# A retention layer with an FP4-quantized linear branch on one core: quantizing the linear weight one tile per body over two groups, and adding two groups' linear output in the last phase

## The chip, the core and the metric

One Trainium2 chip, one of its cores. The metric is the device time of one execution in microseconds, as the median of several. Names in what follows: TensorE (PE in the profile) multiplies, VectorE (DVE) and GpSimd (POOL) work on tiles elementwise, ScalarE (ACT) applies functions, and SyncE (SP) issues all the DMAs of this kernel on one queue, in order.

## What is computed

For x of shape (4, 1024, 1024), taken as 4096 rows of 1024:

```python
xn = layernorm(x)
q, k, v = heads((xn@Wq + bq)*scale), heads(xn@Wk + bk), heads(xn@Wv + bv)   # 16 heads of 64
ret = (q @ k^T) * D            # D: causal, exp(decay * distance)
ret = ret / clip(abs(sum(ret)), 1)
attn = group_norm(ret @ v) * gn_w + gn_b
attention = (silu(xn@Wg + bg) * attn) @ Wo + bo
# linear branch: both operands rounded to FP4 in blocks of 16, with an 8-bit scale per block
linear = dequant(quant_fp4(xn)) @ dequant(quant_fp4(W_f))^T + b_f
out = x + attention + linear
```

The scale of the quantized weight depends on the largest element of the whole weight, so no tile of it can be quantized before all of it has been seen once.

## The kernel before, in words

The 4096 rows are 8 groups of 512 (`GROUP`), and each group is worked in 4 bodies (`CH`). A body of group g does three things side by side. It projects and attends four heads of group g (`project`, `scores`, `state_increments`, `attend_within`, `attend_earlier` on TensorE). It finishes 128 rows of group g-1: the output projection in two halves (`finish_half`, 24 matmuls of 128x512 each) and the linear branch in two halves (`finish_linear`, 8 matmuls each). And it prepares 128 rows of group g+1 (`layernorm`, `quantize_scales`, `quantize_half` on VectorE).

Every engine runs its own program, written out by hand, and semaphores join them. `at(name, phase, body, k)` gives the count that a semaphore has at a point of the program: `PER[name]` holds how often it is raised in the start and in each body of each phase, and `w(name, k)` waits for what was there at the body's start plus k more. The order of the calls in each `body` is the order on that engine.

The phases are START, FIRST (group 0), SECOND (group 1), MIDDLE (groups 2 to 7) and TAIL (4 short bodies that finish group 7). The linear weight is 8 tiles of 128 rows of W_f. Its largest element is found in FIRST. In SECOND each body loads, quantizes and transposes two tiles (`load_f`, `f_scales`, `f_half`, `move_f`), and no body of SECOND has a `finish_linear`, because the weight isn't complete. So the linear branch of group 0 is missing from the rows that SECOND stores. It is added in TAIL: the last group prepares the quantized rows of group 0 a second time (in `xqT[:, 0]`), TensorE multiplies them into the two banks `sc`, SP loads the stored rows of `out` into `xt`, VectorE adds (`late_full`, `late_added`, `late_ready`), and SP stores them again.

On VectorE, where the tiles of SECOND stand among the rest matters. A body of SECOND runs: layernorm, quantization of the rows, `f_scales(0)`, `mask_scores(0)`, `f_half(0)`, `states(0)`, `f_half(1)`, `group_norm(0)`, `f_scales(1)`, `mask_scores(1)`, `f_half(0)`, `states(1)`, an `emit_half`, `group_norm(1)`, `emit_half`, `emit_done`, `f_half(1)`. `mask_scores(u)` releases `state_increments(u)` on TensorE, `states(u)` releases `attend_earlier(u)`, and `group_norm(u)`, through `normalize(u)` on ScalarE, releases `transpose_g(u)`. `group_norm(1)` itself waits for `attend_earlier(1)`, the last work of TensorE in a body of SECOND.

Of the kernel before, what the change touches and what calls it, by code (L numbers as in the profile page):

```python
# [73 lines left out]
START, FIRST, SECOND, MIDDLE, TAIL = range(5)  # L74
BODIES = (0, CH, CH, CH * (GROUPS - 2), CH)
# [7 lines left out]
    "scores_full": (0, 2, 2, 2, 0), "probs_ready": (1, 2, 2, 2, 0),  # L83
    "kq_split": (0, 4, 4, 4, 0), "qdec_ready": (0, 2, 2, 2, 0),
    "attn_full": (1, 2, 2, 2, 0), "gstats": (0, 2, 2, 2, 0), "within": (0, 2, 2, 2, 0), "normed": (1, 2, 2, 2, 0),
    "gated": (1, 2, 2, 2, 0), "y_ready": (1, 2, 2, 2, 0),
    "xn_ready": (4, 1, 1, 1, 0), "xq_ready": (1, 1, 1, 1, 0),
    "xhi_ready": (8, 1, 1, 1, 0), "xlo_ready": (1, 1, 1, 1, 0), "xT_full": (8, 0, 0, 0, 0), "xnT_ready": (8, 0, 0, 0, 0),
    "f_max": (1, 2, 0, 0, 0),
    "res_biased": (0, 0, 1, 1, 1), "out_ready": (0, 0, 1, 1, 1), "late_full": (0, 0, 0, 0, 2), "late_added": (0, 0, 0, 0, 2), "late_ready": (1, 0, 0, 0, 1),  # L90
    "xqf_ready": (0, 0, 2, 0, 0), "xqf_moved": (1, 0, 2, 0, 0), "f_loaded": (0, 2, 2, 0, 0),

    "xq_moved": (1, 1, 1, 1, 0), "x_moved": (1, 2, 2, 2, 0),
    "x_loaded": (1, 1, 1, 1, 1), "res_loaded": (0, 0, 1, 1, 1),
    "out_stored": (1, 0, 1, 1, 1), "late_stored": (1, 0, 0, 0, 1),
    "w_k": (0, 2, 2, 2, 0), "w_v": (0, 2, 2, 2, 0), "w_q": (0, 2, 2, 2, 0), "w_g": (0, 2, 2, 2, 0),

    "step": (23, 82, 128, 84, 0),
# [32 lines left out]
def run_phase(eng, phase, body):  # L131

    if phase == MIDDLE:
        for g in range(GROUPS - 2):
            with eng.Fori(0, CH) as q:
                body(MIDDLE, q + g * CH, g % 2, q, g + 2)
    elif phase == FIRST:
        for i in range(CH):
            body(FIRST, i, 0, i, 0)
    else:  # L140
        group = {SECOND: 1, TAIL: GROUPS}[phase]
        with eng.Fori(0, BODIES[phase]) as i:
            body(phase, i, group % 2, i, group)


def build(nc, a):
    with ExitStack() as ctx:
# [138 lines left out]
        def _(sp):  # L286
            for name in PRIMED_SP:
                sp.sem_inc(s[name], 16)

# [27 lines left out]
            def body(phase, i, parity, q, group):  # L317
                w = waiter(sp, phase, i)
                rows = ds(group * GROUP - GROUP + q * P, P) if phase != FIRST else None

# [47 lines left out]
                if phase == TAIL:  # L368
                    w("attn_full", 0)
                    w("res_biased", 0)  # L370
                    sp.dma_start(late_res, a["x"][rows, :]).then_inc(s["res_loaded"], 16)

                    w("late_stored", 0)
                    sp.wait_ge(s["x_loaded"], at("x_loaded", TAIL, 0, 0))
                    sp.dma_start(xt[:], a["out"][ds(q * P, P), :]).then_inc(s["x_loaded"], 16)
                    w("late_ready", 1)
                    sp.dma_start(a["out"][ds(q * P, P), :], xt[:]).then_inc(s["late_stored"], 16)
                    w("out_ready", 1)
                    sp.dma_start(a["out"][rows, :], res[:]).then_inc(s["out_stored"], 16)
                    return  # L380
                if phase == FIRST:
# [43 lines left out]
                    return  # L425
                w("out_stored", 0)
                sp.dma_start(res[:], a["x"][rows, :]).then_inc(s["res_loaded"], 16)
                if phase == SECOND:
                    w("f_max", 0)
                    load_f(0)  # L430
# [34 lines left out]
            for phase in (FIRST, SECOND, MIDDLE, TAIL):  # L465
# [7 lines left out]
        def _(pool):  # L473
# [78 lines left out]
        def _(act):  # L552
# [185 lines left out]
        def _(dve):  # L738
            for name in PRIMED_DVE:
                dve.sem_inc(s[name], 1)  # L740
            here = {"phase": START, "body": 0, "n": 0, "scale_n": 0}
# [221 lines left out]
            def body(phase, i, parity, q, group):  # L963
# [196 lines left out]
        def _(pe):  # L1160
# [276 lines left out]
```

## Time and profile before

| | before |
|---|---|
| median of 3 runs | 2232.05 us (2230.95 to 2232.88) |
| profiled execution: its own time | 2231.07 us |
| profiled execution: span | 2228.9 us |
| PE busy | 2093.5 us (94%) |
| DVE busy | 1534.4 us (69%) |
| ACT busy, POOL busy | 689.3 us, 641.3 us |
| mean granted TensorE clock | 0.972 |

The span is what the profile covers; the 2.2 us between it and the execution's own time lie around it. PE is the matmul engine, and the shares are averages over phases with different limits. In the page's forty slices PE is at 9 tenths or more from the twelfth slice on, and DVE is at 9 tenths from the eighth to the eleventh, which are the slices of SECOND.

### The profile page before, as it was taken

The numbers are of one execution on the slowest core, as the hardware profiler recorded it, in microseconds if no ns is written. First come the engines' busy times: TensorE is split into PE (matmuls) and PEld (weight loads), VectorE is DVE, ScalarE is ACT, GpSimd is POOL, SyncE is SP. The second block draws the span as 40 slices with busy tenths as digits, with TensorE's granted clock in tenths as the row PEclk, the third lists the DMA queues.
The fourth block names the chain that finished last, engine by engine and source line by source line (L and its number), as shares of the span: only waits on it lengthen the run. The fifth ranks groups of instructions, "written<-read, shape, count | busy, mean of one in ns | idle before, by whom it ended". The sixth has DMA issues, their size and how long they took to land.

```text
span 2228.9 us, 51250 instructions
## 1 busy us (share of the span) xinstructions
PE 2093.5 (94%) x18047; PEld 1066.7 (48%) x18098; DVE 1534.4 (69%) x4379; ACT 689.3 (31%) x1318; POOL 641.3 (29%) x456
## 2 busy tenths in 40 slices
PE   5687888989899999999999999999999999999999
PEld 3343444444454545555545455554554555545444
DVE  8587878999966666666676766666666666666742
ACT  5555451322133223222322322223222322322210
POOL 1222232233232332223332232332332223323321
PEclk8888999999899999999999999999999999999999
DMA  7656733432333332323333233233333322333323
GB/s 309 214 190 219 258 110 95 144 108 91 94 119 118 101 106 90 100 89 104 118 110 109 90 99 108 77 118 118 108 108 90 99 90 94 119 118 99 104 75 123
DMA packets 180244, 269.30 MB, mean 121 GB/s; under 512 B 117184, under 2 KB 117312, under 8 KB 180160
## 3 DMA queue, kind: packets, MB, share of 16 engines
q1 hardware_dynamic: 180160, 268.19, 37.7%
q8 instruction: 51, 0.84, 0.2%
q14 instruction: 33, 0.27, 0.0%
HBM read 201.04 MB, written 37.75 MB: 107 GB/s over the span
## 4 chain that ended last, share of the span: by engine, by line
PE 74%; DVE 17%; DMA 3%; issue 2%; ACT 1%; SPq 1%; POOL 0%; DVEq 0%; ACTq 0%
PE mm L1257 46%; PE mm L1199 7%; PE tp L1199 7%; PE mm L1208 4%; DMA ftile<-in_w_f 2%; PE tp L1267 2%; PE four L1307 2%; PE four L1320 2%; PE tp L1295 1%; DVE xa L807 1%; PE four L1280 1%; DVE xa L808 1%; DVE state L1004 1%; DVE xa L802 1%; DVE wo L896 1%
## 5 line engine op out<-in xcount | busy, mean ns | idle before, releaser
L1257 PE MATMUL mm<-xnT,wring 128*128 128x512 f16 x6144 | 1379.2, 383 | 14.4 <-ACT qT L620 14.1
L1257 PEld LDWEIGHTS mm<-xnT,wring 128*128 128x128 f16 x6144 | 603.1, 99 | 720.3 <-issue 44.1
L651 ACT ACTIVATE work<-four,gs 128x64 f32<-128x64 f32 x512 | 158.5, 414 | 575.5 <-DVE gs L1031 575.5
L512 POOL TENSOR_TENSOR yT<-gn,gate 128x512 f32 (+1 forms) x64 | 82.8, 1293 | 881.2 <-ACT gn L662 881.2
L1018 DVE BATCH_NORM_STATS2 gst<-four 128x6 f32<-128x64 f32 x512 | 73.6, 217 | 215.4 <-PE four L1320 215.4
L1199 PE MATMUL mm<-wo,yT 128*128 128x512 f16 x864 | 194.1, 381 | 0.1
L495 POOL TENSOR_TENSOR qparts<-qT,qparts 128x512 f16<-128x512 f32 x64 | 78.5, 1227 | 372.0 <-ACT qT L620 371.8
L495 POOL TENSOR_TENSOR kparts<-kT,kparts 128x512 f16<-128x512 f32 x64 | 83.0, 1297 | 234.5 <-ACT kT L620 234.5
L1199 PE MATMUL tp<-wo,yT 128*128 128x512 f16 x672 | 149.6, 379 | 0.0
L1199 PEld LDWEIGHTS mm<-wo,yT 128*128 (+1 forms) x864 | 82.3, 98 | 98.7 <-issue 1.9
L620 ACT ACTIVATE vT<-mm,consts,down 128x512 f32<-128x512 f32 x64 | 49.8, 778 | 230.4 <-PE mm L1257 230.4
L618 ACT ACTIVATE qparts<-mm,consts,down 128x512 f16<-128x512 f32 x64 | 49.7, 776 | 226.2 <-PE mm L1257 226.2
L1199 PEld LDWEIGHTS tp<-wo,yT 128*128 (+1 forms) x672 | 65.8, 98 | 79.2
L1208 PE MATMUL mm<-wf,xqT 128*128 128x512 bf16 x368 | 88.4, 381 | 7.6 <-issue 7.6
L618 ACT ACTIVATE kparts<-mm,consts,down 128x512 f16<-128x512 f32 x64 | 50.7, 792 | 140.8 <-PE four L1280 139.5
L807 DVE TENSOR_TENSOR xa<-xa,xm 128x512 f32<-128x512 f32 x80 | 92.1, 1151 | 2.8
L1000 DVE COPY state<-tp 128x65 f32<-128x65 f32 x32 | 7.2, 225 | 117.6 <-PE four L1295 117.6
L1002 DVE COPY state<-carry 128x65 f32 x32 | 8.1, 254 | 116.1 <-PE four L1295 114.1
L502 POOL TENSOR_TENSOR qT<-qT,qfac 128x512 f32<-128x512 f32 x64 | 82.1, 1283 | 11.6 <-POOL qparts L495 11.0
L513 POOL TENSOR_TENSOR gate<-gn,gate 128x512 f32<-128x512 f32 x64 | 83.2, 1300 | 0.0
L620 ACT ACTIVATE gate<-mm,consts,down 128x512 f32<-128x512 f32 x64 | 51.0, 796 | 96.9 <-PE mm L1257 96.9
L1307 PE MATMUL four<-v,probs 64*64 64x65 f32 x2048 | 80.4, 230 | 0.0
(194 smaller groups left out, 2710.5 us busy)
## 6 DMA issues: line engine op xcount, KB each, us to landing
wring<-parts SPq DMA_DIRECT2D x252, 512.0 KB, 3.5
xt<-in_x SPq DMA_DIRECT2D x34, 512.0 KB, 3.6
out<-res SPq DMA_DIRECT2D x32, 512.0 KB, 3.0
parts<-wo SPq DMA_DIRECT2D x28, 512.0 KB, 8.1
res<-in_x SPq DMA_DIRECT2D x28, 512.0 KB, 3.6
ftile<-in_w_f SPq DMA_DIRECT2D x16, 512.0 KB, 4.7
parts<-wring SPq DMA_DIRECT2D x8, 512.0 KB, 7.1
probs<-in_x SPq DMA_DIRECT2D x5, 512.0 KB, 3.8
```

Source lines behind the costliest of these rows:

```text
L495: nc.gpsimd.tensor_tensor(parts[:, 1], full, parts[:, 0], ALU.subtract)\
L502: nc.gpsimd.tensor_tensor(qT[:, u].rearrange("p (c t) -> p c t", c=CH), qT[:, u].rearrange("p (c t) -> p c t", c=CH), factor, ALU.mult).th ...
L512: nc.gpsimd.tensor_tensor(hi, gn[:], gate[:, u], ALU.mult)
L513: nc.gpsimd.tensor_tensor(gate[:, u], gn[:], gate[:, u], ALU.mult).then_inc(s["gated"], 1)
L618: nc.scalar.activation((kparts, None, qparts)[n][:, 0], mm[0][:], ACT.Identity, bias=bias[:, n, pair(u)], scale=down[:, n, pair(u)])
L620: nc.scalar.activation(dst, mm[n % 2][:], ACT.Silu if n == 3 else ACT.Identity, bias=bias[:, n, pair(u)], scale=down[:, n, pair(u)])\
L651: last = nc.scalar.activation(work[:, c * P + h * HD:c * P + (h + 1) * HD], ao[h][:, c * VW:c * VW + HD], ACT.Identity, bias=gs[:, 1, g:g ...
L807: then(V.tensor_tensor(xa[:], xa[:], xm[:], ALU.add))
L1199: last = MM(out[:], y[:, yj, k, ds(q * P, P)], wo[:, wj, k, h * GROUP:(h + 1) * GROUP], start=(n == 0), stop=(n == 3 * KT - 1))
L1208: last = MM(out, xs[:, k, :], wf[:, k, h * GROUP:(h + 1) * GROUP], start=(k == 0), stop=(k == KT - 1))
L1257: last = MM(mm[n % 2][:], wring[:, n, wj, k, :], xnT[:, parity, xj, k, :], start=(j == 0), stop=(j == 3 * KT - 1))
L1307: last = MM(ao[h][tokens(k), columns(k)], probs[tokens(k), h, k // 2, 0:SUB], v1[tokens(k), k // 2, h, :], start=(k < 2), stop=False, skip ...
```

## The change

The weight is quantized one tile per body, over two groups: SECOND (group 1) and a new phase THIRD (group 2); MIDDLE has groups 3 to 7. A body of SECOND or THIRD on VectorE has one `f_scales`, one `f_half(0)` and one `f_half(1)`, at the places that the first tile had, and nothing at those of the second. THIRD has no `finish_linear`, so that group 1 too lacks its linear branch when it is stored. TAIL now adds it for groups 0 and 1. The quantized rows of group 1 are kept for that: SP writes `xqT[:, 1]` (1 MB) to DRAM at the start of SECOND and reads it back after the last body of MIDDLE, into a part of `xnT` that is free by then. A body of TAIL multiplies 16 matmuls into `sc` and 16 into `ao`, and loads, adds and stores two sets of rows, one in `xt` and one in `ftile`. In all, TensorE has as many matmuls as before.

```diff
+START, FIRST, SECOND, THIRD, MIDDLE, TAIL = range(6)
+QUANTIZE = (SECOND, THIRD)
+BODIES = (0, CH, CH, CH, CH * (GROUPS - 3), CH)
...
-"late_full": (0, 0, 0, 0, 2), "late_added": (0, 0, 0, 0, 2), "late_ready": (1, 0, 0, 0, 1),
-"xqf_ready": (0, 0, 2, 0, 0), "xqf_moved": (1, 0, 2, 0, 0), "f_loaded": (0, 2, 2, 0, 0),
+"late_full": (0, 0, 0, 0, 0, 4), "late_added": (0, 0, 0, 0, 0, 4), "late_ready": (2, 0, 0, 0, 0, 2), "late_loaded": (0, 0, 0, 0, 0, 2),
+"xqf_ready": (0, 0, 1, 1, 0, 0), "xqf_moved": (1, 0, 1, 1, 0, 0), "f_loaded": (0, 2, 1, 1, 0, 0),
...
+"out_stored": (1, 0, 1, 1, 1, 1), "late_stored": (2, 0, 0, 0, 0, 2),
...
+late_x = [xqT[:, 0], xnT[:, 1, 0].rearrange("p k t -> p (k t)").bitcast(BF16).rearrange(
+    "p (c k t) -> p c k t", c=CH, k=KT)]
+late_bufs = [xt, ftile]
+late_banks = [sc, ao]
... SP, TAIL
-w("late_stored", 0)
-sp.wait_ge(s["x_loaded"], at("x_loaded", TAIL, 0, 0))
-sp.dma_start(xt[:], a["out"][ds(q * P, P), :]).then_inc(s["x_loaded"], 16)
-w("late_ready", 1)
-sp.dma_start(a["out"][ds(q * P, P), :], xt[:]).then_inc(s["late_stored"], 16)
+for j in range(2):
+    late_rows = a["out"][ds(q * P + j * GROUP, P), :]
+    w("late_stored", j)
+    if j == 0:
+        sp.wait_ge(s["x_loaded"], at("x_loaded", TAIL, 0, 0))
+    sp.dma_start(late_bufs[j][:], late_rows).then_inc(s["late_loaded"], 16)
+    w("late_ready", j + 1)
+    sp.dma_start(late_rows, late_bufs[j][:]).then_inc(s["late_stored"], 16)
... SP, between the phases
+if phase == SECOND:
+    sp.wait_ge(s["xq_moved"], at("xq_moved", SECOND, 0, 0))
+    sp.dma_start(a["xq1"], xqT[:, 1].rearrange("p c k t -> p (c k t)")).then_inc(xq1_kept, 16)
+if phase == THIRD:
+    sp.wait_ge(xq1_kept, 16)
+if phase == TAIL:
+    sp.wait_ge(s["attn_full"], at("attn_full", TAIL, 0, 0))
+    sp.dma_start(late_x[1].rearrange("p c k t -> p (c k t)"), a["xq1"]).then_inc(xq1_back, 16)
... DVE, TAIL
+for j in range(2):
+    w("late_loaded", j + 1)
+    w("late_full", 2 * j + 2)
+    for h in range(2):
+        o = half(late_bufs[j], h)
+        V.scalar_tensor_tensor(o, late_banks[j][h], ffn_scale, o, ALU.mult, ALU.add)\
+         .then_inc(s["late_added"], 1)
+    w("late_added", 2 * j + 2)
+    V.tensor_copy(ls[:, 18:19], ls[:, 15:16]).then_inc(s["late_ready"], 1)
... DVE, bodies that quantize
 group_norm(0)
-if phase == SECOND:
-    f_scales(1)
 mask_scores(1)
-if phase == SECOND:
-    f_half(0)
 states(1)
...
-if phase == SECOND:
+if phase in QUANTIZE:
     emit_half(w, 1, "mm1", 5)
     emit_done(w, "mm1_free", 5)
-    f_half(1)
... PE, TAIL
 pe.wait_ge(s["xq_moved"], i * 16 + at("xq_moved", TAIL, 0, 1 - CH))
-w("late_ready", 0)
-linear(sc[0], 1 - parity, q, 0).then_inc(s["late_full"], 1)
-if last_g:
-    transpose_g(1, 1)
-linear(sc[1], 1 - parity, q, 1).then_inc(s["late_full"], 1)
+pe.wait_ge(xq1_back, 16)
+pe.wait_ge(s["normed"], at("normed", TAIL, 0, 0))
+for j in range(2):
+    w("late_ready", j)
+    for h in range(2):
+        linear(late_banks[j][h], late_x[j], q, h).then_inc(s["late_full"], 1)
+    if last_g and j == 0:
+        transpose_g(1, 1)
 finish_linear(w, parity, q, 0, "mm1", 1)
```

On VectorE, the end of a body of SECOND and the start of the next, where before had the second half of the second tile. Before:

```order
L1138 SCALAR_TENSOR_TENSOR res<-mm,cols,res 128x512 [waits mm1_full]
L1152 COPY ls<-ls 128x1 [waits mm1_free]
L802 TENSOR_TENSOR xa<-ftile,qs 128x512
L751 REGISTER_ALU
L803 TENSOR_SCALAR xa<-xa 128x512 [waits step]
L751 REGISTER_ALU
L805 TENSOR_SCALAR xm<-xa 128x512 [waits step]
```

After:

```order
L1155 SCALAR_TENSOR_TENSOR res<-mm,cols,res 128x512 [waits mm1_full]
L1169 COPY ls<-ls 128x1 [waits mm1_free]
L143 REGISTER_ALU
L143 COMPARE_AND_BRANCH
L143 UNCONDITIONAL_BRANCH
L143 ISA
L790 BN_STATS ls<-xt 128x6 [waits x_loaded]
```

The layernorm of the next body (`BN_STATS`) now follows `emit_done` (the `COPY`) at once; before, the seven operations of `f_half(1)` stood between.

On TensorE, the second body of TAIL (`four` is the tile of the banks `sc` and `ao`). Before:

```order
L1208 MATMUL four<-wf,xqT 128x512 [waits late_ready,xq_moved]
L1208 MATMUL four<-wf,xqT 128x512 x15
L1208 MATMUL mm<-wf,xqT 128x512 [waits xqf_moved,mm1_free]
L1208 MATMUL mm<-wf,xqT 128x512 x7
L1208 MATMUL tp<-wf,xqT 128x512 [waits xqf_moved,t1_free]
L1208 MATMUL tp<-wf,xqT 128x512 x7
```

After:

```order
L1225 MATMUL four<-wf,xqT 128x512 [waits normed,late_ready,xq1_back,xq_moved]
L1225 MATMUL four<-wf,xqT 128x512 x15
L1225 MATMUL four<-wf,xnT 128x512 [waits late_ready]
L1225 MATMUL four<-wf,xnT 128x512 x15
L1225 MATMUL mm<-wf,xqT 128x512 [waits xqf_moved,mm1_free]
L1225 MATMUL mm<-wf,xqT 128x512 x7
```

Sixteen matmuls more, with a wait on `late_ready` of their own ahead of them.

On SP, from the last body of MIDDLE through TAIL. Before:

```order
L345 DMA_TRANSPOSE xqT<-xq 128x8x128
L135 REGISTER_ALU
L135 COMPARE_AND_BRANCH
L142 UNCONDITIONAL_BRANCH
L282 REGISTER_ALU [waits attn_full]
L371 ISA [waits res_biased]
L371 DMA probs<-in_x 128x1024
```

After:

```order
L354 DMA_TRANSPOSE xqT<-xq 128x8x128
L136 REGISTER_ALU
L136 COMPARE_AND_BRANCH
L484 DMA xnT<-xq 128x4096 [waits attn_full]
L143 UNCONDITIONAL_BRANCH
L289 REGISTER_ALU [waits attn_full]
L380 ISA [waits res_biased]
L380 DMA probs<-in_x 128x1024
```

The 1 MB load of the kept rows stands behind the last transposing DMA and ahead of the loads of TAIL.

## Rows read from the trace of the kernel before

**Rows 1.** Busy time by stretch, one body each; columns named, PEclk is the clock.

```profile
core 0: us, PE busy (x) PEld busy (x) DVE busy (x) ACT busy (x) POOL busy (x), PEclk, DMA share, GB/s
316.50:386.70 70.20, 63.81 (x554) 32.42 (x552) 63.26 (x162) 18.58 (x37) 20.96 (x15) 0.95 0.31 91
...
460.40:534.00 73.60, 63.69 (x556) 32.75 (x552) 67.11 (x169) 18.58 (x37) 21.05 (x14) 0.94 0.36 110
...
738.10:802.20 64.10, 63.78 (x559) 32.45 (x560) 41.68 (x125) 18.57 (x37) 19.73 (x14) 1.00 0.33 102
```

**Rows 2.** Timeline of PE, second body of SECOND: start, duration, operation, idle before.

```profile
460.42 11.40 PE L1257 MATMUL mm<-xnT,wring 128*128 128x512 f16 x48
...
499.09 0.28 PE L1295 MATMUL tp<-v,kn 64*64 64x65 f32 x2 [4.63 <-DVE probs L988]
...
532.96 1.15 PE L1320 MATMUL four<-state,qT 64*64 64x65 f32 x32 [5.09 <-DVE carry L1006]
```

**Rows 3.** Timeline of PE, first body of SECOND.

```profile
316.48 10.53 PE L1257 MATMUL mm<-xnT,wring 128*128 128x512 f16 x48
...
350.79 0.28 PE L1295 MATMUL tp<-v,kn 64*64 64x65 f32 x2 [1.13 <-DVE probs L988]
...
371.32 0.65 PE L1229 MATMUL tp<-consts,work 128*128 128x128 f32 x4 [0.89 <-ACT work L651]
```

**Rows 4.** Timeline of PE, third body of MIDDLE.

```profile
738.11 10.52 PE L1257 MATMUL mm<-xnT,wring 128*128 128x512 f16 x48
...
771.21 0.28 PE L1295 MATMUL tp<-v,kn 64*64 64x65 f32 x2
...
790.72 0.60 PE L1229 MATMUL tp<-consts,work 128*128 128x128 f32 x4
...
802.21 4.05 PE L1257 MATMUL mm<-xnT,wring 128*128 128x512 f16 x18
```

**Rows 5.** Timeline of DVE in the first two bodies of SECOND.

```profile
321.39 1.29 DVE L770 BATCH_NORM_STATS2 ls<-xt 128x6 f32<-128x512 f32 x2
...
349.88 0.76 DVE L988 TENSOR_TENSOR probs<-four,dmask 128x256 f32<-128x256 f32 x2 [0.41 <-DVE qs L793]
...
466.07 0.68 DVE L802 TENSOR_TENSOR xa<-ftile,qs 128x512 f32<-128x512 f32 x1
...
470.23 1.28 DVE L770 BATCH_NORM_STATS2 ls<-xt 128x6 f32<-128x512 f32 x2
...
498.19 0.76 DVE L988 TENSOR_TENSOR probs<-four,dmask 128x256 f32<-128x256 f32 x2 [0.41 <-DVE qs L793]
```

**Rows 6.** Stretches of 3 us: length, PE busy, granted clock, DMA share, GB/s.

```profile
349.00:352.00 3.00, 1.87 (x61) 1.00 0.98 337
...
500.00:503.00 3.00, 3.00 (x33) 0.50 0.50 205
```

**Rows 7.** Timeline of PE, after a long idle time in FIRST, and in TAIL.

```profile
215.34 7.56 PE L1257 MATMUL mm<-xnT,wring 128*128 128x512 f16 x24 [5.96 <-ACT qT L620]
...
2148.53 1.89 PE L1208 MATMUL four<-wf,xqT 128*128 128x512 bf16 x8
2154.26 0.65 PE L1229 MATMUL tp<-consts,work 128*128 128x128 f32 x4 [3.84 <-ACT work L651]
...
2172.19 3.40 PE L1208 MATMUL four<-wf,xqT 128*128 128x512 bf16 x15
...
2189.46 2.75 PE L1208 MATMUL four<-wf,xqT 128*128 128x512 bf16 x12
```

**Rows 8.** Timeline of SP's queue and DVE in TAIL.

```profile
2156.01 0.34 SPq L371 DMA_DIRECT2D probs<-in_x  x1
...
2160.95 1.41 DVE L971 SCALAR_TENSOR_TENSOR xt<-four,cols,xt 128x512 f32<-128x512 f32 x2 [7.48 <-DMA xt<-out]
...
2182.12 0.35 SPq L377 DMA_DIRECT2D out<-xt  x1
...
2198.96 0.35 SPq L377 DMA_DIRECT2D out<-xt  x1
```

More of the change, by code:

```diff
@@ L69 @@
 NCONST = sum(n for _, n in CONST_WIDTHS)
-START, FIRST, SECOND, MIDDLE, TAIL = range(5)
-BODIES = (0, CH, CH, CH * (GROUPS - 2), CH)
+START, FIRST, SECOND, THIRD, MIDDLE, TAIL = range(6)
+QUANTIZE = (SECOND, THIRD)
+BODIES = (0, CH, CH, CH, CH * (GROUPS - 3), CH)
 PER = {
[4 rows of a table removed]
[L83 to L90, printed above, removed]
-    "xqf_ready": (0, 0, 2, 0, 0), "xqf_moved": (1, 0, 2, 0, 0), "f_loaded": (0, 2, 2, 0, 0),
[L93 to L98, printed above, removed]
[4 rows of a table added]
+    "scores_full": (0, 2, 2, 2, 2, 0), "probs_ready": (1, 2, 2, 2, 2, 0),
+    "kq_split": (0, 4, 4, 4, 4, 0), "qdec_ready": (0, 2, 2, 2, 2, 0),
+    "attn_full": (1, 2, 2, 2, 2, 0), "gstats": (0, 2, 2, 2, 2, 0), "within": (0, 2, 2, 2, 2, 0), "normed": (1, 2, 2, 2, 2, 0),
+    "gated": (1, 2, 2, 2, 2, 0), "y_ready": (1, 2, 2, 2, 2, 0),
+    "xn_ready": (4, 1, 1, 1, 1, 0), "xq_ready": (1, 1, 1, 1, 1, 0),
+    "xhi_ready": (8, 1, 1, 1, 1, 0), "xlo_ready": (1, 1, 1, 1, 1, 0), "xT_full": (8, 0, 0, 0, 0, 0), "xnT_ready": (8, 0, 0, 0, 0, 0),
+    "f_max": (1, 2, 0, 0, 0, 0),
+    "res_biased": (0, 0, 1, 1, 1, 1), "out_ready": (0, 0, 1, 1, 1, 1), "late_full": (0, 0, 0, 0, 0, 4), "late_added": (0, 0, 0, 0, 0, 4), "late_ready": (2, 0, 0, 0, 0, 2), "late_loaded": (0, 0, 0, 0, 0, 2),
+    "xqf_ready": (0, 0, 1, 1, 0, 0), "xqf_moved": (1, 0, 1, 1, 0, 0), "f_loaded": (0, 2, 1, 1, 0, 0),
+    "xq_moved": (1, 1, 1, 1, 1, 0), "x_moved": (1, 2, 2, 2, 2, 0),
+    "x_loaded": (1, 1, 1, 1, 1, 0), "res_loaded": (0, 0, 1, 1, 1, 1),
+    "out_stored": (1, 0, 1, 1, 1, 1), "late_stored": (2, 0, 0, 0, 0, 2),
+    "w_k": (0, 2, 2, 2, 2, 0), "w_v": (0, 2, 2, 2, 2, 0), "w_q": (0, 2, 2, 2, 2, 0), "w_g": (0, 2, 2, 2, 2, 0),
+    "step": (23, 82, 106, 104, 84, 0),
@@ L133, in run_phase @@
     if phase == MIDDLE:
-        for g in range(GROUPS - 2):
+        for g in range(GROUPS - 3):
             with eng.Fori(0, CH) as q:
-                body(MIDDLE, q + g * CH, g % 2, q, g + 2)
+                body(MIDDLE, q + g * CH, (g + 3) % 2, q, g + 3)
     elif phase == FIRST:
@@ L140, in run_phase @@
     else:
-        group = {SECOND: 1, TAIL: GROUPS}[phase]
+        group = {SECOND: 1, THIRD: 2, TAIL: GROUPS}[phase]
         with eng.Fori(0, BODIES[phase]) as i:
@@ L247, in build @@
         x_in = [ctx.enter_context(nc.semaphore(f"x_in{j}")) for j in range(CH)]
+        xq1_kept = ctx.enter_context(nc.semaphore("xq1_kept"))
+        xq1_back = ctx.enter_context(nc.semaphore("xq1_back"))
         bias_sum = ctx.enter_context(nc.semaphore("bias_sum"))
@@ L288, in _ @@
                 sp.sem_inc(s[name], 16)
+            sp.sem_inc(s["late_stored"], 16)
             def load_raw(b, c):
@@ L319, in body @@
                 rows = ds(group * GROUP - GROUP + q * P, P) if phase != FIRST else None
+                f_rows = ds(q * (2 * P) + (phase - SECOND) * P, P) if phase in QUANTIZE else None
                 def load_x(ahead):
@@ L425, in body @@
                     return
+                if phase in QUANTIZE:
+                    sp.wait_ge(s["f_max"], at("f_max", SECOND, 0, 0))
                 w("out_stored", 0)
                 sp.dma_start(res[:], a["x"][rows, :]).then_inc(s["res_loaded"], 16)
-                if phase == SECOND:
-                    w("f_max", 0)
-                    load_f(0)
+                if phase in QUANTIZE:
+                    load_f()
                     load_slice(0, 0)
@@ L464, in _ @@
                 store_parts(0, c)
-            for phase in (FIRST, SECOND, MIDDLE, TAIL):
+            for phase in (FIRST, SECOND, THIRD, MIDDLE, TAIL):
+                if phase == SECOND:
[6 more added lines that the diff above has]
+                    sp.dma_start(late_x[1].rearrange("p c k t -> p (c k t)"), a["xq1"]).then_inc(xq1_back, 16)
                 run_phase(sp, phase, body)
@@ L542, in body @@
                 gate_y(0)
-                if phase == SECOND:
+                if phase in QUANTIZE:
                     add_biases()
                 gate_y(1)
-            for phase in (FIRST, SECOND, MIDDLE, TAIL):
+            for phase in (FIRST, SECOND, THIRD, MIDDLE, TAIL):
                 run_phase(pool, phase, body)
@@ L730, in first_group @@
                 normalize(1)
-            for phase in (FIRST, SECOND, MIDDLE):
+            for phase in (FIRST, SECOND, THIRD, MIDDLE):
                 run_phase(act, phase, body)
@@ L740, in _ @@
                 dve.sem_inc(s[name], 1)
+            dve.sem_inc(s["late_ready"], 1)
             here = {"phase": START, "body": 0, "n": 0, "scale_n": 0}
@@ L1098, in body @@
                 quantize_half(xt, 1)
-                if phase == SECOND:
-                    f_scales(0)
+                if phase in QUANTIZE:
+                    f_scales()
                 mask_scores(0)
-                if phase == SECOND:
+                if phase in QUANTIZE:
                     f_half(0)
                 states(0)
-                if phase == SECOND:
+                if phase in QUANTIZE:
                     f_half(1)
                 group_norm(0)
-                if phase == SECOND:
-                    f_scales(1)
                 mask_scores(1)
-                if phase == SECOND:
-                    f_half(0)
                 states(1)
@@ L1117, in body @@
                 group_norm(1)
-                if phase == SECOND:
+                if phase in QUANTIZE:
                     emit_half(w, 1, "mm1", 5)
                     emit_done(w, "mm1_free", 5)
-                    f_half(1)
                 if phase == MIDDLE:
@@ L1154, in _ @@
             run_phase(dve, FIRST, body)
-            for phase in (SECOND, MIDDLE, TAIL):
+            for phase in (SECOND, THIRD, MIDDLE, TAIL):
                 run_phase(dve, phase, body)
@@ L1202, in finish_half, with linear @@
                 last.then_inc(s[f"{bank}_full"], 1)
-            def linear(out, parity, q, h):
-                xs = xqT[:, 1 - parity, ds(q, 1)].rearrange("p a k t -> p (a k) t")
+            def linear(out, x_quantized, q, h):
+                xs = x_quantized[:, ds(q, 1)].rearrange("p a k t -> p (a k) t")
                 for k in range(KT):
@@ L1215, in finish_linear @@
                 pe.wait_ge(s["xqf_moved"], at("xqf_moved", MIDDLE, 0, 0))
-                linear(banks[bank][:], parity, q, h).then_inc(s[f"{bank}_full"], 1)
+                linear(banks[bank][:], xqT[:, 1 - parity], q, h).then_inc(s[f"{bank}_full"], 1)
             def body(phase, i, parity, q, group, last_g=True):
@@ L1377, in _ @@
             pe.wait_ge(lo_done, SLICES * BATCHES)
-            run_phase(pe, SECOND, body)
-            run_phase(pe, MIDDLE, body)
+            for phase in (SECOND, THIRD, MIDDLE):
+                run_phase(pe, phase, body)
             for i in range(BODIES[TAIL]):
```

32 lines of the change are left out of this document (12 added, 20 removed), and 8 rows, old and new, of the table PER.

## The prediction, made before the changed kernel ran

> **What bounds the kernel now.** I read the busy time by body first, then the timelines of TensorE and VectorE around the waits, and the last phase by SP's queue. A body of MIDDLE takes 64.1 us, in which TensorE is busy for 63.8 and VectorE for 41.7: TensorE bounds it [rows 1]. A body of SECOND takes 70.2 (the first) or 73.6 us, though it lacks the 16 matmuls of `finish_linear`, and VectorE is busy for 63 to 67 us of it [rows 1]. Two waits of TensorE make the difference: 4.63 us ahead of `state_increments(0)`, for `mask_scores(0)`, and 5.09 us ahead of `attend_earlier(1)`, for `states(1)` [rows 2]. After such a wait the granted clock stands at 0.50, the lower of its two levels (1.2 GHz), for about 3 us [rows 6]. In TAIL a body is TensorE alone: it runs from 2171.97 to 2189.24 (one matmul of 0.216 us before each row shown, whose record is missing), 17.27 us for 80 matmuls, 0.216 us each [rows 7]. What the change moves is thus VectorE work out of SECOND, matmuls out of group 2, and both into TAIL.
>
> **Group 1 and group 2, before.** SECOND starts at 316.48 [rows 3], the third body of MIDDLE at 738.11 [rows 4], and two more bodies of 64.1 complete group 2: 738.11 + 128.2 - 316.48 = 549.8 us for eight bodies.
>
> **The same eight bodies after.** The floor of one is a MIDDLE body without its 16 matmuls: 64.1 - 16 x 0.216 = 60.6 us. Does VectorE keep it? I follow its chain from the body's start.
> - `group_norm(1)`, `emit_half` and `emit_done` end 466.07 - 460.42 = 5.65 us after the start of a body whose clock is low [rows 2, 5]; at the full clock I take 5.5. Then `f_half(1)` came, 470.23 - 466.07 = 4.16 us, which is gone.
> - Layernorm to `mask_scores(0)`, with one `f_scales` in it, took 28.0 us in the second body and 28.5 in the first [rows 5]. I take 28.0. `state_increments(0)` starts 0.9 us after `mask_scores(0)` (350.79 against 349.88 [rows 3, 5]), so 5.5 + 28.0 + 0.9 = 34.4 us into the body. MIDDLE has it at 771.21 - 738.11 = 33.1 [rows 4]. So TensorE still waits, by 1.3 us in a body instead of 4.63. The first body of SECOND has exactly this shape already (no `f_half(1)` ahead of it) and shows a wait of 1.13 us [rows 3].
> - From there to `transpose_g(0)` MIDDLE takes 19.5 us [rows 4]; the first body of SECOND takes 371.32 - 350.79 = 20.5, with 0.89 us of waiting for `normalize(0)`, because `f_half(0)` and `f_half(1)` stand ahead of `group_norm(0)` [rows 3]. These stay, so I take 20.5.
> - From `transpose_g(0)` to the end MIDDLE takes 802.21 - 790.72 = 11.5 us with 16 matmuls of the linear branch, so 8.0 without [rows 4]. The wait of 5.09 us goes: `mask_scores(1)` comes right after `group_norm(0)`, and `states(1)` has nothing of the weight ahead of it. What is late next there is TensorE itself.
>
> A body is 34.4 + 20.5 + 8.0 = 62.9 us; the first, which has no `emit_half` ahead, is 34.3 + 20.5 + 8.0 = 62.8. Sum: 62.8 + 7 x 62.9 = 503.1 us. The first body of MIDDLE after THIRD waits some 0.5 us for bank mm1, which `emit_half` frees 5.5 us into the body while TensorE wants it after 24 matmuls, 5.2 us; inside the bodies above this wait is covered by the one at `state_increments(0)`. **Saved: 549.8 - 503.1 - 0.5 = 46.2 us.** The floor of 60.6 in all eight would save 549.8 - 485 = 65; if the low clock came once in each of seven bodies (3 us at half rate lose 1.5 us [rows 6], of which 1.0 shows, since the wait for `normalize(0)` shrinks), it would be 39. In the first body of SECOND the clock was at 1.00 in and after its 1.13 us wait [rows 6], so I take no loss.
>
> The other edits of these phases cost nothing that I can see: the 1 MB store of the quantized rows goes out at the start of SECOND, ahead of SP's load of `res` and of the weight tile, which is read only some 30 us later (`f_scales` ends at 349.5 [rows 5]), and the queue moves about a third of what it could there (DMA share 0.31 [rows 1]). If it did hold them up, 3 us of 30 are used.
>
> **TAIL, entry.** Before, TensorE did one linear half (to 2150.3), waited for `normed`, and went on at 2154.26 [rows 7]. Now nothing of TAIL starts before `xq1_back`. The load stands on SP behind `out_ready` and the transposing DMA, where before the load of `probs` was, at 2156.01 [rows 8]. Two loads of 512 KB issued from 2156.01 on were both used by VectorE at 2160.95, so 1 MB took 4.9 us [rows 8]; I take 2161.0 for the start. TensorE has then idled for 12 us. After an idle time of 5.96 us 24 matmuls took 7.56 us in place of 5.3 [rows 7]: 2.2 us lost to the clock, which I take for each long wait (the wait of 3.84 us, the nearest lower row, cost 1.7: from it to 2171.97 are 17.7 us for 72 matmuls, 15.55, and four transposes, some 0.4).
>
> The Trainium skill, DMA: Bandwidth & Descriptors, section Measured, gives 6.15 us for 1 MB. By that figure the start would be at 2162.2 and the whole sum 1.2 us longer; the trace's two loads speak against it here.
>
> **TAIL, the wait inside a body.** The diff and the order show what decides: the matmuls into `ao` (j = 1) wait for `late_ready` at count 2 + 2i + 1, and the semaphore is primed with 2. So they wait until VectorE has added j = 0 of the same body, not of the body before. That add waits for rows that SP loads only after it has stored the rows of the body before. Before, SP issued the store that follows the add at 2182.12 and 2198.96, that is 10.15 and 9.72 us after the starts 2171.97 and 2189.24 [rows 7, 8]; nobody but SP waited for it. Now TensorE does, at 16 matmuls or 3.45 us into the body, until 9.9 + 0.1 = 10.0: 6.55 us of waiting in bodies 1 to 3. Behind it stand the 80 matmuls that a body had before, 17.27 us, and 2.2 of low clock. A body: 10.0 + 17.3 + 2.2 = 29.5 us in place of 17.3, three times 12.2 = 36.6 us. The second add's load (issued once the first store has landed) is not waited for by TensorE within the body.
>
> Body 0: from 2161.0, 16 matmuls 3.45 and clock 2.2, VectorE's adds 1.41 and its copy with the semaphores 0.55 [rows 8], to 2168.6; then 17.3, to 2185.9, against 2172.0 before: 13.9 us. The end after the last matmul is as before. **TAIL costs 36.6 + 13.9 = 50.5 us** (13.8 of them are the 64 matmuls moved). Without the low clock it is 41.7, with twice the loss 59; I take the middle, and 47 to 55 as the likely span.
>
> **The sum.** 50.5 - 46.2 = +4.3 us. The profiled execution took 2231.07 us by its own time (span 2228.9), so 2235.4; the median of before stands 1.0 us higher, so about 2236.
>
> **Rivals.** (a) Also slower, by more: the low clock strikes in the quantizing bodies too. Their waits of about 1 us come twice a body, and the row at 1.00 [rows 6] is of one such wait alone. Seven bodies at +1.0 us give +11 in all, 2243; with VectorE held longer by GpSimd up to 2249. (b) Faster: VectorE meets GpSimd's operations less than in the first body of SECOND, where the row from layernorm to mask took 0.5 us more than in the second [rows 5]. If neither wait remains above 0.3 us, the eight bodies take 8 x 61.2 = 490 us, the saving is 59 and the time 2232.05 + 50.5 - 59 = 2223. It decides at 61.8 us a body (8 x 61.8 = 494, saving 55): below, the change is faster by over 0.2%. (c) The waits in TAIL are not there, since SP's load could run ahead of the matmuls: TAIL would cost 13.9 + 3 x 3.45 = 24 us, and the time would be 2210. The order of SP's queue speaks against it. (d) The gain and the loss cancel closely (seven bodies of 62.4 give 3.5 us more, a loss of 1.7 in place of 2.2 us to the clock in four places 2.0 more): -1 us, 2229 to 2233.
>
> **How the numbers follow.** The forecast, +1 to +8 us, gets 0.48; (a) and beyond 0.22; (b) 0.12; (c) 0.03; (d) 0.15. A measurement of this kernel can tell 0.2%, 4.5 us, from no change, and a little less than half of the forecast's span lies below that. So faster 0.12 + 0.03 = 0.15, same 0.15 + 0.22 = 0.37, slower 0.26 + 0.22 = 0.48. The range leaves out (c), most of (b) and the top of (a): 2226 to 2248.
>
> **What would show it.** In the timeline of the changed kernel, bodies of SECOND and THIRD near 62.9 us, with a wait of about 1 us for `probs` and one for `work`, and none for `carry` ahead of `attend_earlier(1)`; TensorE idle from 2148.6 less what was saved for 12 us, the first matmul of TAIL following the landing of `xnT<-xq1`; in each later body of TAIL a wait of 6 to 7 us between the 16th and 17th matmul, ended by VectorE's copy, and 29 us from body to body. The forecast is wrong if the quantizing bodies have clocks below 1.00 throughout, or if the wait in TAIL is under 4 us.

## The result and the profile after

| | before | after |
|---|---|---|
| median, runs on the same chips | 2231.09 us (6 runs) | 2242.39 us (2239.96 to 2245.6, 6 runs) |
| ratio to before, 95% interval | | 1.0051 (1.0038 to 1.0064) |
| profiled execution, its own time | 2231.07 us | 2245.6 us |
| its span | 2228.9 us | 2243.6 us |

The change makes the kernel slower by 0.51%, about 11 us. The sum had given +4.3 us, with "slower by over 0.2%" at 0.48; the range, 2226 to 2248, holds the time. The 11 us lie outside the +1 to +8 us of the forecast itself, where rival (a) had its figure. The profiled execution is the slowest of the six, so its ledger comes to 14.7 us and not to 11.3:

| stretch | before | after | difference | forecast |
|---|---|---|---|---|
| start to SECOND | 316.5 | 319.0 | +2.5 | 0 |
| groups 1 and 2, eight bodies | 549.8 | 509.3 | -40.5 | -46.7 |
| five groups of MIDDLE | 1282.2 | 1282.3 | +0.1 | +0.5 |
| TAIL to the end of the span | 80.4 | 133.0 | +52.6 | +50.5 |

The first line belongs to no edit: in the ten profiled executions of this study, before, after and the eight experiments, SECOND starts between 315.0 and 320.2 us.

Bodies by stretch, the same view as [rows 1] (length, busy time of PE, PEld, DVE, ACT, POOL, granted clock, DMA share, GB/s): two of SECOND, one of THIRD, one of MIDDLE.

```profile
446.70:510.60 63.90, 61.17 (x553) 30.78 (x554) 51.93 (x148) 18.57 (x37) 19.94 (x14) 1.00 0.37 115
510.60:574.40 63.80, 61.12 (x552) 30.70 (x552) 51.83 (x147) 18.58 (x37) 19.94 (x14) 1.00 0.37 115
...
701.40:764.90 63.50, 61.14 (x545) 30.72 (x546) 51.33 (x146) 18.58 (x37) 20.21 (x14) 1.00 0.37 116
...
892.80:956.90 64.10, 64.10 (x569) 32.49 (x568) 42.03 (x126) 18.57 (x37) 19.62 (x14) 1.00 0.32 102
```

A quantizing body went from 73.6 us to 63.8 in SECOND and 63.5 in THIRD. VectorE is busy for 52 of them in place of 67, and the clock stays at 1.00 where it was 0.94. The timeline of PE in the fourth body shows what is left of the waits of [rows 2]:

```profile
510.57 10.76 PE L1277 MATMUL mm<-xnT,wring 128*128 128x512 f16 x48 [0.64 <-DVE res L1155]
...
545.11 0.28 PE L1315 MATMUL tp<-v,kn 64*64 64x65 f32 x2 [1.13 <-DVE probs L1010]
...
565.63 0.65 PE L1246 MATMUL tp<-consts,work 128*128 128x128 f32 x4 [0.88 <-ACT work L670]
...
574.43 0.82 PE L1277 MATMUL mm<-xnT,wring 128*128 128x512 f16 x3 [0.64 <-DVE res L1155]
```

4.63 has become 1.13 and 5.09 is gone. The wait for `work` of [rows 3] is there in every body, with 0.88 us in SECOND and 0.43 to 0.47 in THIRD. And there is one that the forecast didn't have: 0.64 us at the start of the body, for bank mm0. Its cause stands in the timeline of POOL and DVE just before:

```profile
571.24 2.35 POOL L546 TENSOR_TENSOR res<-res,out_bias 128x1024 f32<-128x1024 f32 x1
573.63 0.75 DVE L1155 SCALAR_TENSOR_TENSOR res<-mm,cols,res 128x512 f32<-128x512 f32 x1 [3.68 <-POOL res L546]
```

VectorE's `emit_half` empties bank mm0 into `res`, and waits 3.68 us for GpSimd's `add_biases`, which in a quantizing body stands between its two `gate_y`. In the kernel before VectorE came to this add only after it was done, since `states(1)` was late:

```profile
526.39 2.79 POOL L527 TENSOR_TENSOR res<-res,out_bias 128x1024 f32<-128x1024 f32 x1
...
532.73 0.75 DVE L1138 SCALAR_TENSOR_TENSOR res<-mm,cols,res 128x512 f32<-128x512 f32 x1
```

There the add ends at 529.2 and VectorE needs it at 532.7: a margin of 3.5 us, which the change used up.

TAIL, timeline of PE: its first work, and the bodies 1 and 2 (compare [rows 7]).

```profile
2123.33 6.24 PE L1225 MATMUL four<-wf,xqT 128*128 128x512 bf16 x16 [12.51 <-DMA xnT<-xq]
...
2148.54 3.62 PE L1225 MATMUL four<-wf,xqT 128*128 128x512 bf16 x16
2158.88 5.55 PE L1225 MATMUL four<-wf,xnT 128*128 128x512 bf16 x16 [6.72 <-DVE ls L996]
...
2178.08 3.62 PE L1225 MATMUL four<-wf,xqT 128*128 128x512 bf16 x16
2188.68 6.01 PE L1225 MATMUL four<-wf,xnT 128*128 128x512 bf16 x16 [6.99 <-DVE ls L996]
```

TensorE stands still for 12.51 us until the kept rows are back. Bodies take 29.5, 30.3 and 30.2 us, and in each a wait of 6.4 to 7.0 us, ended by VectorE's copy, parts the first 16 matmuls from the next 16, which then take 5.6 to 6.6 us in place of 3.6. SP's queue and DVE show why the wait is so long (compare [rows 8]):

```profile
2151.55 0.35 SPq L380 DMA_DIRECT2D probs<-in_x  x1
2152.24 0.35 SPq L387 DMA_DIRECT2D xt<-out  x1
2157.22 1.41 DVE L993 SCALAR_TENSOR_TENSOR xt<-four,cols,xt 128x512 f32<-128x512 f32 x2 [6.67 <-DMA xt<-out]
```

The load of the rows to be added goes out 3.7 us into the body, behind the store of the body before, and VectorE can't add before 8.7 us. The clock, in stretches of 3 us of that body (length, PE busy, clock, DMA share, GB/s):

```profile
2152.00:2155.00 3.00, 0.16 (x1) 1.00 1.00 305
2155.00:2158.00 3.00, 0.00 (x0) 0.67 0.35 141
2158.00:2161.00 3.00, 2.12 (x6) 0.50 0.43 175
2161.00:2164.00 3.00, 3.00 (x11) 0.70 0.45 104
```

It falls within the idle time. It is 0.50, 1.2 GHz, in the stretch in which the work comes back at 2158.88, and 0.70 in the next; the 16 matmuls take 5.55 us in place of 3.62.

### The profile page after: what moved, and what is told of

It reads as the page before. It is cut to its first block, busy times and chain, and to the rows that moved or that the text cites. A ratio compares the mean times of both kernels' runs of the same rounds, so it can differ in the third digit from the quotient of the medians.

```text
span 2243.6 us, 51233 instructions
## 1 busy us (share of the span) xinstructions
PE 2097.7 (93%) x18098; PEld 1058.1 (47%) x18098; DVE 1521.0 (68%) x4375; ACT 688.5 (31%) x1318; POOL 639.8 (29%) x456
## 4 chain that ended last, share of the span: by engine, by line
PE 63%; DVE 23%; issue 4%; DMA 4%; ACT 2%; POOL 2%; SPq 2%; DVEq 0%; ACTq 0%; POOLq 0%
PE mm L1277 39%; PE mm L1216 6%; PE tp L1216 6%; PE mm L1225 3%; DMA ftile<-in_w_f 2%; DVE xa L827 2%; PE tp L1287 2%; PE four L1327 2%; DVE xa L828 2%; DVE xa L822 1%; PE four L1225 1%; PE four L1340 1%; DVE xm L826 1%; DVE xa L823 1%; DVE xm L825 1%
## 5 line engine op out<-in xcount | busy, mean ns | idle before, releaser
L1216 PE MATMUL mm<-wo,yT 128*128 128x512 f16 x960 | 214.0, 379 | 0.1
L1216 PEld LDWEIGHTS mm<-wo,yT 128*128 (+1 forms) x960 | 91.0, 98 | 108.2
L1216 PE MATMUL tp<-wo,yT 128*128 128x512 f16 x576 | 128.2, 379 | 0.0
L1216 PEld LDWEIGHTS tp<-wo,yT 128*128 (+1 forms) x576 | 56.4, 98 | 68.0
L1225 PE MATMUL mm<-wf,xqT 128*128 128x512 bf16 x352 | 83.6, 380 | 0.0
L534 POOL TENSOR_TENSOR yT<-gate,yT 128x512 f32 (+1 forms) x64 | 75.7, 1182 | 11.4 <-POOL gate L532 10.8
L539 POOL TENSOR_TENSOR xhl<-xt,xhl 128x1024 f16<-128x1024 f32 x32 | 77.4, 2417 | 0.0
```

What stands on the lines that cost most here:

```text
L539: nc.gpsimd.tensor_tensor(xhl[:, 1], xt[:], xhl[:, 0], ALU.subtract).then_inc(s["xlo_ready"], 1)
L1216: last = MM(out[:], y[:, yj, k, ds(q * P, P)], wo[:, wj, k, h * GROUP:(h + 1) * GROUP], start=(n == 0), stop=(n == 3 * KT - 1))
L1225: last = MM(out, xs[:, k, :], wf[:, k, h * GROUP:(h + 1) * GROUP], start=(k == 0), stop=(k == KT - 1))
```

## The experiments

The theory: SECOND and THIRD save some 40 us, held below what they could by VectorE's order and GpSimd's late bias add, and TAIL gives back 52, through a wait whose count is one too high and a load that stands too late on SP's queue. The rival: the quantizing bodies save little, or TAIL is bound by its own loads and adds. Times are medians of 4 to 10 runs; each ratio is to the kernel before on the same chip. Each edit is to the changed kernel, unless it says more.

**The quantizing part alone.** TAIL is as before, and THIRD still leaves out its linear branch, so this kernel leaves out the linear branch of group 1 altogether: it serves to time the rest. The loops of SP and VectorE in TAIL run once, the counts are lowered to match, and the 1 MB load back is left out. On TensorE:

```diff
-pe.wait_ge(xq1_back, 16)
-pe.wait_ge(s["normed"], at("normed", TAIL, 0, 0))
-for j in range(2):
-    w("late_ready", j)
-    for h in range(2):
-        linear(late_banks[j][h], late_x[j], q, h).then_inc(s["late_full"], 1)
-    if last_g and j == 0:
-        transpose_g(1, 1)
+w("late_ready", 0)
+linear(sc[0], late_x[0], q, 0).then_inc(s["late_full"], 1)
+if last_g:
+    transpose_g(1, 1)
+linear(sc[1], late_x[0], q, 1).then_inc(s["late_full"], 1)
```

> The changed kernel without group 1's linear branch in TAIL: 64 matmuls, four loads, adds and stores and the 1 MB load back are left out, and TAIL is that of before. Theory A (the quantizing bodies save 40 us, TAIL gives back 52): 2231.1 - 40.5 + 0.4 = 2191 us. Rival B (the quantizing bodies save little, the moved matmuls are the loss): about 2242.4 - 13.8 = 2229 us.

Measured: 2190.78 us, ratio 0.9817 (0.9796 to 0.9839). That is theory A to a fraction of a microsecond, and 38 us from the rival; theory A took its figures from the ledger above, so this confirms that the ledger's two parts add up. So the second late set in TAIL costs 51.6 us, of which its matmuls are 13.8.

**The count of one wait.**

```diff
 for j in range(2):
-    w("late_ready", j)
+    w("late_ready", j - 1)
```

> Only TensorE's wait on late_ready in TAIL is one count lower, so that it waits for the add that last read the same bank, in the body before, and not for the add of j = 0 of this body. Theory A (this wait is the loss in TAIL): bodies 1 to 3 go from 30.0 us to 96 x 0.216 = 20.7 us, body 0 gains 1.3: 2242.4 - 29 = 2213 us, faster than before. Rival B (SP's queue and VectorE's adds bound a body of TAIL as well, so the wait moves to a bank or a load): bodies near 26 us, 2229 us.

Measured: 2215.53 us, ratio 0.9922 (0.9901 to 0.9943). The timeline of PE, starts of the bodies 1 and 2 of TAIL:

```profile
2122.13 6.18 PE L1225 MATMUL four<-wf,xqT 128*128 128x512 bf16 x16 [12.52 <-DMA xnT<-xq]
...
2146.06 3.40 PE L1225 MATMUL four<-wf,xqT 128*128 128x512 bf16 x15
2149.30 3.62 PE L1225 MATMUL four<-wf,xnT 128*128 128x512 bf16 x16
...
2166.78 3.40 PE L1225 MATMUL four<-wf,xqT 128*128 128x512 bf16 x15
```

A body is 20.72 us, 96 matmuls of 0.216, without a wait. SP's chain of loads, adds and stores fits under it, but for the very end: the last rows leave 6.1 us after the last matmul in place of 5.1, since VectorE's last late add waits for its load. The wait at the entry is untouched. One number in the code was worth 27 us, and turns the change from a loss into a gain of 0.8%.

**The load back earlier.** SP's last body of MIDDLE is taken out of its loop so that the load can stand in it, and the load at TAIL's start is taken out. TensorE's waits for it and for `normed` move behind the first late set, so two things change at once:

```diff
 for n in range(4):
     load_slice(1, n)
+if last:
+    sp.dma_start(late_x[1].rearrange("p c k t -> p (c k t)"), a["xq1"]).then_inc(xq1_back, 16)
 w("out_ready", 1)
... PE, TAIL
-pe.wait_ge(xq1_back, 16)
-pe.wait_ge(s["normed"], at("normed", TAIL, 0, 0))
 for j in range(2):
     w("late_ready", j)
+    if j:
+        pe.wait_ge(xq1_back, 16)
+        pe.wait_ge(s["normed"], at("normed", TAIL, 0, 0))
     for h in range(2):
         linear(late_banks[j][h], late_x[j], q, h).then_inc(s["late_full"], 1)
-    if last_g and j == 0:
-        transpose_g(1, 1)
+        if last_g and j == 0 and h == 0:
+            transpose_g(1, 1)
```

> The 1 MB load back is issued in the last body of MIDDLE right behind its last weight slice, some 17 us earlier, and the first late half is ahead of the waits for it and for normed again, as before. Theory A (the entry wait of 12.5 us is the load's place on SP's queue): the long wait falls to the 3.8 us of before, but the wait on late_ready in body 0 grows from 1.3 to some 5 us, since the add needs the rows of out: 4 to 5 us gained, 2238 us. Rival B (the entry is held by the load's length or by memory traffic): no gain, 2242 us.

Measured: 2237.91 us, ratio 1.0025 (1.0015 to 1.0035). Timeline of PE at the entry:

```profile
2115.88 1.11 PE L1255 MATMUL tp<-consts,work 128*128 128x128 f32 x4 [3.84 <-ACT work L679]
2116.78 3.62 PE L1234 MATMUL four<-wf,xqT 128*128 128x512 bf16 x8
2124.24 5.60 PE L1234 MATMUL four<-wf,xnT 128*128 128x512 bf16 x16 [3.84 <-DVE ls L1005]
```

As expected: the wait of 12.5 us is one of 3.84, as before the change, and a second one of 3.84 for the add stands behind it (some 5 were expected), since the count of the wait is as in the changed kernel. It was the load's place, not its length: issued at 2093.37, it took 5.8 us and had landed some 11 us before TAIL began, so TensorE would not have waited for it in either order.

**The scales behind the mask.**

```diff
-if phase in QUANTIZE:
-    f_scales()
 mask_scores(0)
 if phase in QUANTIZE:
+    f_scales()
     f_half(0)
```

> In the eight quantizing bodies f_scales stands behind mask_scores(0) and not ahead of it. Theory A (VectorE's chain through group_norm(0) sets the body, and TensorE's waits for probs and for work are shares of one lag): the wait of 1.14 us for probs goes and the wait of 0.88 us for work grows by the same, 2242 us. Rival B (each wait costs by itself): 8 x 1.14 = 9 us gained, 2233 us.

Measured: 2236.11 us, ratio 1.0013 (1.0004 to 1.0023), between the two theories. PE in the fourth body:

```profile
551.05 0.70 PE L1339 MATMUL four<-state,qT 64*64 64x65 f32 x32 [0.48 <-DVE carry L1028]
...
564.22 0.65 PE L1245 MATMUL tp<-consts,work 128*128 128x128 f32 x4 [0.86 <-ACT work L670]
573.03 10.76 PE L1276 MATMUL mm<-xnT,wring 128*128 128x512 f16 x48 [0.65 <-DVE res L1154]
```

The wait for `probs`, 1.13, is gone; 0.48 of it comes back ahead of `attend_earlier(0)`, and the wait for `work` is as it was. (In THIRD 0.15 to 0.27 comes back there, and the wait for `work` grows from 0.45 to 0.80.) The eight bodies take 504.3 us in place of 509.3: more than half of rival B's 9 us is gained, where theory A had none. What became of it stands on VectorE, in the fourth body of the changed kernel and then of this one:

```profile
541.16 0.52 DVE L805 TENSOR_SCALAR qs<-qs,cols 128x64 f32<-128x64 f32 x1
...
558.24 1.14 DVE L1040 BATCH_NORM_STATS2 gst<-four 128x6 f32<-128x64 f32 x8
```

```profile
541.05 0.25 DVE L805 TENSOR_SCALAR qs<-qs,cols 128x64 f32<-128x64 f32 x1
...
556.82 1.14 DVE L1040 BATCH_NORM_STATS2 gst<-four 128x6 f32<-128x64 f32 x8
```

VectorE reaches `group_norm(0)` 47.0 us after the start of the body in place of 47.7, and these 0.65 us are all that the body gains. They are 0.3 of the 0.41 us that it idled between `f_scales` and `mask_scores(0)` [rows 5], 0.27 of an operation of `f_scales` that no longer runs beside a GpSimd one, and 0.1 in `f_half(1)`. So the chain up to `group_norm(0)` sets the body and the waits are shares of one lag, as theory A has it; its forecast of no gain fails because the edit also shortens that chain.

**The pieces of the tile spread.**

```diff
-if phase in QUANTIZE:
-    f_scales()
 mask_scores(0)
 if phase in QUANTIZE:
-    f_half(0)
+    f_scales()
 states(0)
 if phase in QUANTIZE:
-    f_half(1)
+    f_half(0)
 group_norm(0)
 mask_scores(1)
+if phase in QUANTIZE:
+    f_half(1)
 states(1)
```

> In the quantizing bodies the weight's three pieces stand where VectorE has idle time: f_scales behind mask_scores(0), f_half(0) behind states(0), f_half(1) behind mask_scores(1). Theory A (VectorE has room for one tile a body, and only the pieces ahead of mask_scores(0) and group_norm(0) hold TensorE): no wait for probs or work, bodies of 60.6 + 0.65 for bank mm0 = 61.3 us in place of 63.7: 19 us gained, 2223 us. Rival B (the lag moves to states(1) and attend_earlier(1), as it did in the kernel before): bodies near 63 us, 2236 us.

Measured: 2224.76 us, ratio 0.9973 (0.9961 to 0.9985). Timeline of PE, two successive body starts:

```profile
499.74 10.76 PE L1277 MATMUL mm<-xnT,wring 128*128 128x512 f16 x48 [0.64 <-DVE res L1155]
...
561.33 10.76 PE L1277 MATMUL mm<-xnT,wring 128*128 128x512 f16 x48 [0.64 <-DVE res L1155]
```

61.6 us a body, 492.7 us for the eight; the waits for `probs`, `work` and `carry` are gone, and the one for bank mm0 is the only one left. VectorE has room for one tile a body, and where its pieces stand decides whether TensorE pays.

**The bias add earlier.**

```diff
 split(3, kT[:], kparts)
-if phase == MIDDLE:
+if phase != FIRST:
     add_biases()
...
 gate_y(0)
-if phase in QUANTIZE:
-    add_biases()
 gate_y(1)
```

> In the quantizing bodies GpSimd adds the biases behind its third split, as in MIDDLE, and no longer between its two gate_y. Theory A (the wait of 0.65 us for bank mm0 at the start of each body comes from GpSimd's late add, which VectorE's emit_half waits for): the wait goes, 8 x 0.65 = 5 us gained, 2238 us. Rival B (at its new place the 2.3 us add holds VectorE's two-input operations in f_scales, which stand on the path): the bank wait goes, but the wait for probs grows by 1.5 to 2 us a body, 2250 us.

Measured: 2261.7 us, ratio 1.0134 (1.0119 to 1.015). The sign is rival B's and the size larger than its figure: 19 us lost where it had some 8. Timeline of DVE, POOL and PE in a body of SECOND:

```profile
546.70 2.35 POOL L546 TENSOR_TENSOR res<-res,out_bias 128x1024 f32<-128x1024 f32 x1
546.83 2.27 DVE L805 TENSOR_SCALAR qs<-qs 128x64 int32<-128x64 int32 x1
...
552.29 0.37 PE L1313 MATMUL tp<-v,kn 64*64 64x65 f32 x2 [3.21 <-DVE probs L1008]
```

The add holds an operation of `f_scales` that takes 0.20 us otherwise, on the path to `mask_scores(0)`. The wait for bank mm0 went, but the wait for `probs` is 3.21 us in place of 1.13, and after it the clock is low again (0.56 from 486 to 489 us, behind the same wait in the body before). So it is in seven of the eight bodies, the first alone keeping 1.00 behind a wait of 3.20 us; in the changed kernel's eight bodies it never is. The eight bodies take 530.6 us.

**Together.** The late count, the early load, the spread pieces and the early bias add; and the same without the last.

> All of it together: the lower count on late_ready, the early load back with the order of before at TAIL's entry, the spread pieces and the early bias add. If the gains add up: 2242.4 - 27 (late count) - 9.7 (entry, which pays in full only with the lower count) - 19 - 5 = 2182 us. If the early bias add costs VectorE what it saves TensorE: 2187 to 2192 us.

> As e7_all with the bias add left where the change has it: 2242.4 - 27 - 9.7 - 19 = 2187 us. The difference to e7_all is what the place of the bias add is worth when nothing of the weight stands on VectorE's path at that point: 5 us if the bank wait goes without a new one.

Measured: 2184.64 us, ratio 0.9788 (0.9775 to 0.9801), and 2186.85 us, ratio 0.9803 (0.979 to 0.9816). The gains add up to within 3 us (2182 and 2187 were forecast). Timeline of PE with all four: a body of SECOND, then the entry and the first two bodies of TAIL.

```profile
500.21 10.70 PE L1285 MATMUL mm<-xnT,wring 128*128 128x512 f16 x48 [0.27 <-issue]
561.33 10.75 PE L1285 MATMUL mm<-xnT,wring 128*128 128x512 f16 x48 [0.23 <-issue]
...
2093.93 1.11 PE L1253 MATMUL tp<-consts,work 128*128 128x128 f32 x4 [3.83 <-ACT work L677]
...
2098.25 4.12 PE L1232 MATMUL four<-wf,xnT 128*128 128x512 bf16 x16
...
2116.02 3.62 PE L1232 MATMUL four<-wf,xqT 128*128 128x512 bf16 x16
...
2136.74 3.62 PE L1232 MATMUL four<-wf,xqT 128*128 128x512 bf16 x16
```

61.1 us a body, half a microsecond above TensorE's floor. The same early bias add that cost 19 us with `f_scales` ahead of the mask takes the eight bodies from 492.7 to 489.1 us here, because it now strikes behind `mask_scores(0)`, where VectorE has slack: an operation of 0.25 us takes 2.16, and TensorE waits for nothing.

```profile
531.41 2.16 DVE L812 TENSOR_SCALAR qs<-qs,cols 128x64 f32<-128x64 f32 x1
```

The medians differ by 2.2 us. Every run of the one lies below every run of the other (2182.9 to 2185.2 against 2185.3 to 2190.3), but the intervals of the two ratios overlap. The version with all four, at 2184.6 us, is 2.1% faster than the kernel before and computes all that it does.

## Why the prediction was right, and where it was off

**What bounds the kernel, and the direction of both sums: right.** The first experiment parts them: without the second late set 2190.8 us, so the quantizing part gains 41 against the kernel before on the same chip, and TAIL takes 52 back.

**VectorE's chain up to `transpose_g(0)`: right.** The forecast had `state_increments(0)` 34.4 us into a body and `transpose_g(0)` 20.5 us after it. They stand at 34.5 and 20.5 (510.57, 545.11, 565.63 in the timeline above); in THIRD the second is 20.1. The clock stayed at 1.00, as was assumed; rival (a) did not happen.

**"From `transpose_g(0)` to the end ... 8.0": the term that was too small.** It measured 8.8 us. It was read from MIDDLE, where GpSimd adds the biases early, and the step says that what is late next there "is TensorE itself". In fact `emit_half(0)` waits for `add_biases`, which the quantizing phases have after `gate_y(0)`: 0.64 us a body. The row was in reach, since GpSimd's add is in SECOND too; it was not late there, because `states(1)` was later. Eight times 0.64 makes 5 of the 6 us by which the saving was overrated. That the wait comes from this add is shown by the two combined kernels: with the early add it is absent, and their eight bodies differ by 3.6 us. That it is worth the whole 5 us in the changed kernel is worked out and not shown, since there the early add cost more elsewhere.

**The entry of TAIL: right within a microsecond.** Forecast 12.4 us of idle time from 2148.6 to 2161.0, measured 12.51. The 1 MB load took 5.5 us from issue to landing, where two loads of half the size had given 4.9. (The step has VectorE use both; one of them is GpSimd's, in use from 2159.78, so the 4.9 stand.) The Trainium skill, DMA: Bandwidth & Descriptors, section Measured, has 6.15 us for 1 MB, as the time that the DMA engines are busy with a load issued from GpSimd; this one is issued from SP. The measurement lies between the two and decides: 5.5 here. It went unnoticed since SP reached the load a little earlier than was assumed.

**The wait inside a body of TAIL: right.** Forecast 6.55 us, measured 6.35 to 6.99. The count read from the code was the whole story, as the second experiment shows. The body is 29.5 to 30.3 us against 29.5: the second 16 matmuls start 10.3, 10.6 and 10.0 us into it against 10.0, and the low clock takes 1.9, 2.4 and 2.9 us in place of 2.2 (6.55 us for 16 matmuls that take 3.62). That is 1.6 of the 2.1 us by which TAIL was underrated.

**The sum.** Two large terms of opposite sign, each right within 15%, left a difference of 4 us where the medians show 11. The errors, 6 us in one and 2 in the other, both went the same way and together are larger than the forecast itself. So the mechanism was right and the size of the sum was not: +11.3 us is outside the forecast's +1 to +8 and is the figure of rival (a), 2243, whose mechanism, a low clock in the quantizing bodies, isn't there. That the range holds the time is owed to the width that a rival gave it, which is luck as far as the number goes. Rival (b), faster, fell by the condition that it named itself: neither wait went below 0.3 us (the least is 0.43). Rival (c) didn't happen, but the experiment on the count gives nearly its time, 2215.5 against 2210.

## What to carry to other kernels

When work is taken off a bounding engine, look at what that engine's longest waits were hiding: here a GpSimd add that had come 3.5 us early cost 0.64 us in each body once the wait above it was gone. When a stage is given a second buffer, write down for each wait which earlier use of that same buffer it must follow; with two buffers one semaphore's count runs twice as fast, and an index that is one too high makes the two work in series. A load that a phase opens with belongs behind the last reader of its destination, not at the phase's first line on the queue.

## What the runs showed of the hardware

An elementwise add of GpSimd holds a VectorE operation with a single input, too: an int32 mask on 128x64 took 2.27 us beside a GpSimd add of 2.35 us, and 0.20 us without it; an f32 one on the same shape took 2.16 in place of 0.25. The Trainium skill, SBUF — State Buffer, section SBUF: two separate sides, describes the port pair that the two share as an exclusive lock, taken for a whole instruction by VectorE operations in a two-port mode or with two inputs in SBUF. The trace agrees with the blocking in its length (the held operation ends at 549.10, the add at 549.05); that this operation runs in such a mode no row shows.

In the changed kernel three waits of 0.4 to 1.2 us in each of eight bodies left the granted clock at 1.00 in every stretch of 3 us, while one of 3.21 us ahead of the same matmuls was followed by a clock of 0.56 in the next stretch. The length of the one wait doesn't settle it: behind 3.20 us in the first body of the early bias add the clock stayed at 1.00, and in the kernel before it was at 0.50 from 375 to 378 us behind waits of 0.89 and 2.44 us, which stand 0.65 us apart. With long waits the clock fell while TensorE was still idle (0.67 over the stretch of 3 us before the work came back).
